# Attention's instruction lists in another order on TensorE, ScalarE and VectorE

## The reference

```python
ln_out = _ln(hidden_states, ln_w, ln_b)
q  = _ln(_fp8_linear_pertensor(ln_out, wq,  ...))      # per head, 128 wide; 16 heads
k  = _ln(_fp8_linear_pertensor(ln_out, wk,  ...))      # 8 groups
v  =     _fp8_linear_pertensor(ln_out, wv,  ...)
core = _gqa(q, k, v)                                    # scores, softmax, values, in batches of 64 rows
qx = _ln(_fp8_linear_pertensor(ln_out, wqx, ...))
kx, vx = split(cond @ w_kv_x);  kx = _ln(kx)
xout = _gqa(qx, kx, vx)
x = x + fp8_linear(concat([core, xout]), wproj)
x = x + moe_ffn(_layernorm(x))                          # router, top 2 of 8 experts, and a shared expert
```

## Time and profile before

| | us |
|---|---|
| median of 3 runs | 1134.46 (1134.02 to 1134.89) |
| the profiled execution | 1130.54 |
| its span | 1128.6 |
| PE busy, share of the span | 989.4, 88% |
| PE weight loads busy | 692.6, 61% |
| DVE busy | 824.0, 73% |
| ACT busy | 716.1, 63% |
| POOL busy | 405.8, 36% |

### The profile page before, as it was taken

The page is one execution under the profiler, slowest core; times in us unless marked ns, Lnnn a source line. Parts: engine busy times, 40 slices in busy tenths (PEclk is TensorE's granted clock), DMA queues, the critical chain, the costliest instruction groups (busy, mean ns, idle before and its releaser), DMA issues. The chain is left out here.

```text
span 1128.6 us, 23597 instructions
## 1 busy us (share of the span) xinstructions
PE 989.4 (88%) x7206; PEld 692.6 (61%) x7207; DVE 824.0 (73%) x1596; ACT 716.1 (63%) x1223; POOL 405.8 (36%) x627
## 2 busy tenths in 40 slices
PE   2447999999999999999999999958999959999994
PEld 1434667667676667666676766746565536666663
DVE  6566888988888888888889888878866634444442
ACT  5967777777777777777777777636455515445452
POOL 3005444444444444444444444400561002332332
PEclk8679999999999999999999999986999979999998
DMA  9245110000100101001010010013453146222222
GB/s 278 50 92 170 43 39 19 27 29 19 37 19 19 37 19 37 19 19 37 19 37 19 19 37 19 1 57 131 150 188 130 56 150 132 28 23 28 28 24 27
DMA packets 32369, 65.20 MB, mean 58 GB/s; under 512 B 3664, under 2 KB 20688, under 8 KB 31952
## 3 DMA queue, kind: packets, MB, share of 16 engines
q1 hardware_dynamic: 23312, 50.20, 13.7%
q0 software_dynamic: 9024, 14.59, 7.6%
HBM read 53.42 MB, written 16.59 MB: 62 GB/s over the span
## 5 line engine op out<-in xcount | busy, mean ns | idle before, releaser
L754 POOL TENSOR_TENSOR root<-vareps,neghalf 128x4 f32<-128x4 f32 (+1 forms) x128 | 169.0, 1320 | 10.0
L747 POOL TENSOR_TENSOR var<-ssq,unit 128x4 f32<-128x4 f32 (+1 forms) x128 | 50.0, 391 | 314.6 <-DVE ssq L659 314.6
L543 PE MATMUL b_pj<-w_hi,xq 128*128 128x512 f16 x384 | 146.6, 382 | 6.6 <-PEq L154 6.3
L559 PE MATMUL b_tr<-ident,nrm 128*128 128x128 f32 x768 | 120.6, 280 | 35.7 <-ACT qT L629 17.4
L543 PE MATMUL b_pj<-w_lo,xq 128*128 128x512 f16 x384 | 146.5, 382 | 0.0
L659 DVE TENSOR_REDUCE ssq<-sq 128x4 f32<-128x512 f32 x192 | 128.5, 681 | 14.9 <-ACT sq L611 14.8
L670 DVE TENSOR_TENSOR nrm<-raw,rstd 128x512 f32<-128x512 f32 x192 | 126.4, 686 | 16.2 <-POOL rstd L758 14.5
L1321 POOL DMA_INDIRECT out<-xg x39 | 60.6, 1553 | 210.7 <-ACT xg L1422 191.4
L559 PEld LDWEIGHTS b_tr<-ident,nrm 128*128 128x128 f32 x768 | 85.5, 146 | 73.0 <-DVE nrm L670 41.0
L569 PEld LDWEIGHTS b_sc<-kT,qT 128*128 128x128 f32 x1024 | 124.3, 192 | 9.3 <-ACT qT L629 0.3
L569 PE MATMUL b_sc<-kT,qT 128*128 128x64 f32 x1024 | 121.3, 272 | 0.0
(11 more groups left out here) (258 smaller groups left out, 2260.8 us busy)
## 6 DMA issues: line engine op xcount, KB each, us to landing
nst<-in_ffw SPq DMA_DIRECT2D x30, 512.0 KB, 3.3
wload<-in_ffw SPq DMA_DIRECT2D x30, 512.0 KB, 3.4
xbuf<-zero SPq DMA_DIRECT2D x39, 129.0 KB, 2.5
xg<-xbuf SPq DMA_DIRECT2D x9, 516.0 KB, 4.2
w<-in_w_all POOLq DMA_DIRECT2D x12, 256.0 KB, 9.2
x_sb<-in_x SPq DMA_DIRECT2D x4, 512.0 KB, 6.8
cstage<-in_ctxT SPq DMA_DIRECT2D x1, 2048.0 KB, 9.6
w<-in_w_all SPq DMA_DIRECT2D x4, 512.0 KB, 14.8
```

The source lines that it names most:

```text
L543: last = pe.matmul(o, a[:, k, bass.ts(i, P)], w[:, k, at:at + BANK], start=(k == 0 and n_ == 0), stop=(k == KT - 1 and n_ == len(terms) - 1))
L559: last = pe.transpose(o, nrm[:, c, hd * P:(hd + 1) * P], ident[:, :])
L754: pool.tensor_tensor(root[:, r % 2, c, :], vareps[:, r % 2, c, :], neghalf[:, 0:1].unsqueeze(2).to_broadcast(shape), ALU.pow).then_inc(s[" ...
```

## The change

Five things are changed, all in the attention.

- PE's list: `pe_probT(0)` moves from behind the second transposes to between the first two projections; `pe_project(2)` moves ahead of the third transposes, so `pe_values` stands directly ahead of the third projection.
- ACT's list: squares and raw copies are separate steps (`act_square` is new), so that `act_exp` stands behind the first raw copy, `act_tev(1)` between the second square and its raw copy, and `act_tev(2)` and `act_ptev` between the third square and its raw copy. The last two copies close the list. `act_weight_squares` goes from the middle to the front and from item N to item N-3.
- DVE's list: `dve_norm(1)` goes ahead of `dve_sub`; `dve_sum` between the first two sums of squares; `dve_cat` and the third sum of squares ahead of `dve_recip`, `dve_norm(0)`, `dve_prob` and `dve_clip`; `dve_round` is last, behind the residual and the statistics, which now belong to item N-3.
- `pe_project` waits for `sq_done` as well (not for c = 1), since a square is no longer always ahead of the copy of another projection.
- `run_slots` runs one slot more at the end, for the steps that are three slots behind.

```diff
--- before.py
+++ after.py
@@ -513,7 +513,7 @@
                         slot(i, r)
                 if before_tail is not None:
                     before_tail()
-                for N in range(4 * (NT - 1), 4 * NT + 2):
+                for N in range(4 * (NT - 1), 4 * NT + 3):
                     slot(N // 4, N % 4)
 
             @block.sync
@@ -531,6 +531,8 @@
                 def step(pe, i, r):
                     n, kind, u = 4 * (4 * i + r) + c, r // 2, r % 2
                     after(pe, "raw_done", n - 1)
+                    if c != 1:
+                        after(pe, "sq_done", NN * (4 * i + r) + max(c - 1, 0))
                     o = b_pj[c % 2][:, :]
                     at = (8 * kind + (u, 2 + 2 * u, 3 + 2 * u, 6 + u)[c]) * BANK
                     if kind == 1 and c in (0, 3):
@@ -600,16 +602,22 @@
                 last.then_inc(s["po_done"], 1)
 
 
+            def act_square(c):
+                def step(act, i, r):
+                    N = 4 * i + r
+                    m = NN * N + c
+                    act.wait_ge(s["proj_done"], 4 * N + c + 1)
+                    after(act, "ssq_done", m - 1)
+                    act.activation(sq[:, (r * NN + c) % 2, :], b_pj[c % 2][:, :], ACT.Square).then_inc(s["sq_done"], 1)
+                return step
+
             def act_raw(c):
                 def step(act, i, r):
                     N = 4 * i + r
                     act.wait_ge(s["proj_done"], 4 * N + c + 1)
                     bk = b_pj[c % 2][:, :]
                     if c < NN:
-                        m = NN * N + c
-                        after(act, "ssq_done", m - 1)
-                        act.activation(sq[:, (r * NN + c) % 2, :], bk, ACT.Square).then_inc(s["sq_done"], 1)
-                        after(act, "norm_done", m - 2 * NN + 1)
+                        after(act, "norm_done", NN * N + c - 2 * NN + 1)
                         act.activation(raw[:, r % 2, c, :], bk, ACT.Copy).then_inc(s["raw_done"], 1)
                     else:
                         after(act, "pv_done", N - 3)
@@ -762,11 +770,37 @@
 
             @block.tensor
             def _(pe):
-                run_slots(pe, [(1, pe_scores), (2, pe_transpose(0)), (3, pe_project(0)), (3, pe_project(1)), (2, pe_transpose(1)), (0, pe_probT), (-1, pe_values), (2, pe_transpose(2)), (3, pe_project(2)), (-2, pe_out), (3, pe_project(3))])
+                run_slots(pe, [
+                    (1, pe_scores),
+                    (2, pe_transpose(0)),
+                    (3, pe_project(0)),
+                    (0, pe_probT),
+                    (3, pe_project(1)),
+                    (2, pe_transpose(1)),
+                    (-1, pe_values),
+                    (3, pe_project(2)),
+                    (2, pe_transpose(2)),
+                    (-2, pe_out),
+                    (3, pe_project(3)),
+                ])
 
             @block.scalar
             def _(act):
-                run_slots(act, [(2, act_tev(0)), (1, act_exp), (3, act_raw(0)), (3, act_raw(1)), (2, act_tev(1)), (0, act_ptev), (2, act_tev(2)), (0, act_weight_squares), (3, act_raw(2)), (3, act_raw(3))])
+                run_slots(act, [
+                    (-3, act_weight_squares),
+                    (2, act_tev(0)),
+                    (3, act_square(0)),
+                    (3, act_raw(0)),
+                    (1, act_exp),
+                    (3, act_square(1)),
+                    (2, act_tev(1)),
+                    (3, act_raw(1)),
+                    (3, act_square(2)),
+                    (2, act_tev(2)),
+                    (0, act_ptev),
+                    (3, act_raw(2)),
+                    (3, act_raw(3)),
+                ])
 
             @block.vector
             def _(dve):
@@ -774,7 +808,24 @@
                     dve.wait_ge(s["st3_done"], EARLY)
                     moments(dve, range(EARLY))
 
-                run_slots(dve, [(1, dve_max), (1, dve_sub), (2, dve_norm(1)), (2, dve_norm(2)), (3, dve_squares(0)), (3, dve_squares(1)), (1, dve_sum), (1, dve_recip), (1, dve_prob), (-1, dve_cat), (-1, dve_clip), (-1, dve_round), (3, dve_squares(2)), (3, dve_norm(0)), (-2, dve_residual), (-2, dve_stats)], early)
+                run_slots(dve, [
+                    (1, dve_max),
+                    (2, dve_norm(1)),
+                    (1, dve_sub),
+                    (2, dve_norm(2)),
+                    (3, dve_squares(0)),
+                    (1, dve_sum),
+                    (3, dve_squares(1)),
+                    (-1, dve_cat),
+                    (3, dve_squares(2)),
+                    (1, dve_recip),
+                    (3, dve_norm(0)),
+                    (1, dve_prob),
+                    (-1, dve_clip),
+                    (-2, dve_residual),
+                    (-3, dve_stats),
+                    (-1, dve_round),
+                ], early)
                 dve.wait_ge(s["st3_done"], NT)
 
             @block.gpsimd
```

## The result

The changed kernel takes 1085.74 us (median of 4, 1085.58 to 1085.91) against 1134.26 for the kernel before in the same comparison: ratio 0.9579, 95% interval 0.9564 to 0.9595, 48.5 us less. In a later comparison it was 1082.86 against 1131.05, ratio 0.9575 (0.9558 to 0.9592); one of the seven executions of the kernel before took 1649 us there at a granted clock of 0.59 and is not counted. The forecast was 1106.5 with a range of 1099 to 1124: the direction was right, the size was too small by 21 us, and the time lies outside the range.

What follows compares the result with a forecast made beforehand. It took a DVE and POOL ring of 10.0 us a slot as the bound; 58 x (10.17 - 9.58) = 34 us, less 6 for short waits, is 28 off 1130.54: 1102.5, as median 1106.5, range 1099 to 1124.

Steps and rivals of the forecast that it cites:

- The ring of DVE and POOL: Attention: POOL's 3.89 us plus DVE's 6.11 from `nrm` to third sum of squares make the 10.0 us slot; 9.29 after.
- POOL's part: From third sum of squares to `nrm`: 3.89 us before, 4.45 after, with POOL held until DVE's `prob` ends.
- the second ring's wait of 17.4 us: PE's transposes waiting for ACT's `qT`; forecast to go, with 0.3 us spare, once a projection lies between.
- rival E: No change, 1134 us: another 10 us ring through exp, square, `qT` and transposes, since `sub` follows a waiting `nrm`; chance 0.05.
- PE's floor after: PE's own work per attention slot after the change: 9.14 us short, 10.00 long, mean 9.58.
- the seam from values to a projection: On PE, in no earlier row, so taken at the 1.24 us of values to transposes; 0.1 either way is 6 us.
- The reserve of 0.1 us a slot: Attention: 6 us of the gain held back for short waits that the timetable does not resolve.
- Filling and draining at nothing, +-3: Both ends of the attention, outside the 58 steady slots: no gain counted, within 3 us either way.
- Rival C: DVE's clip and round hold POOL too: DVE-POOL ring 9.94 us, only 12 us gained, 1123 us; chance 0.20.
- The timetable: Start times within a short slot: norm at 3.33 us in the second, needed by 3.58, so it fits by 0.25.
- Rivals D: Slower, 1145 us: steps moved beside POOL also stretch its `root`; with POOL at 5.5 the slot is 10.35; chance 0.09.
- The edits called free: Side edits expected to cost nothing: probability transposes covered by 2 us; 1.04 us weight squares moved into ACT's 1.49 us wait.

## Why the prediction was too small

**What bounded the kernel before** was half the truth. The ring of DVE and POOL at 10.0 us was there: with DVE's old list no version fell below 1120 except where POOL's part was cut as well (1108). But the ring that set the slot was the other one, through exp, the second `qT` and the third transposes: with 1.43 us cut out of the first, the mean slot stayed at 10.17 (1129.6 us in all), and with the second cut instead, by ACT's list, by PE's, or by both, the first held it at 10.15, 10.09 and 10.03, with PE's weight loads waiting 46 to 52 us for `nrm`. The forecast saw the second ring's wait of 17.4 us and filed it as a minor edit, and gave rival E, which names this ring, 0.05. The price of the whole change was not hurt by that, since it cuts both; any forecast of a part of it from this text would have been wrong, most of all DVE's list alone, 1240 where one ring gives 1107.

**PE's floor after** is the step that failed: forecast 9.14 and 10.00 us, measured 9.01 and 9.87. The term is values, taken at 1.24 from the earlier trace rows, "where nothing is waited for"; it is 1.09. In that row something was waited for. The copy of `qT` ahead of it, in the kernel before:

```profile
464.02 0.80 ACT L629 ACTIVATE qT<-b_tr,col 128x512 f32<-128x512 f32 x1
```

It ends at 464.82, and the transposes start at 464.97, 0.15 behind it. In all 52 slots of the kernel before that were read they start 0.14 or 0.15 behind such a copy, and where they need not wait, with ACT's list alone, they follow values by 1.09 or 1.10. So the 1.24 is 1.09 of values and 0.15 of the wait that the change removes, and the view had no bracket for it. The forecast put its doubt on the seam from values to a projection, at 0.1 to either side; that seam is like the others, and the miss is larger than that bound. The projection behind values takes 0.88 in place of 0.86, which leaves 58 x 0.13 = 7.5 us.

**The reserve of 0.1 us a slot**, 6 us, was for nothing: PE is busy in all of the 548.34 us.

**Filling and draining at nothing, +-3**, was wrong too. Before slot 3 and behind slot 61 another 4.5 + 2.0 us went. The first part is the exchange of third projection and third transposes: with it undone the stretch before slot 3 takes 53.99 us, as long as before (53.52), against 48.92 in the changed kernel measured again. For the second part that exchange does nothing (20.32 us with it undone, 20.09 with it), while PE's whole list undone gives 23.04; which of its entries pays there is open.

28 + 7.5 + 6 + 6.5 = 48, the measured change.

**POOL's part** held: 4.36 us against 4.45, `nrm` and `prob` holding POOL back to back. Rival C fell at the same rows: `root` starts while clip runs and loses 0.07 us beside clip and round. The Trainium skill (GPSIMD Engine Reference, Key points) names instructions in a two-port mode beside those with two SBUF inputs; the kind with two SBUF inputs held POOL here, clip and round did not hold it back. Whether clip and round ran in such a mode is not shown. The timetable was on the safe side: 0.25 us to spare ahead of the second transposes was forecast, and it is 0.50 in the second short slot (scores at 458.54, `nrm` at 461.63, transposes at 462.88, 0.75 needed). Rivals D and E fell with the result. Rival E's ring, through `sub` behind a `nrm` that waits, does exist: it is the 12.4 us of DVE's list alone and the 9.85 of the third transposes put back. In the changed kernel ACT's list and the place of the third projection keep it under PE's 9.01, as the timetable had it.

**The edits called free** were: weight squares, probabilities and `norm` ahead of `sub` change nothing in the changed kernel (1082.7, 1084.1, 1083.7 against 1082.9). Of the change as it is described, what carries it is on PE the third projection ahead of the third transposes, on ACT some part of a list whose old order has exp ahead of all squares and copies of its slot but one, on DVE some part of the list other than the place of `sub`.

## What to carry to other kernels

When an engine waits, follow each of its waits round until the chain comes back to itself, and write down the length of every such ring, also of the one behind the smaller wait: two rings of about 10 us hide each other, and an edit that shortens one may lengthen the other. Before an instruction that waits for a slow neighbour goes ahead of another in a list, ask who hangs on that other: DVE's list alone cost 110 us by this, and 91 of them came back with one exchange. Where the work of the busiest engine is the floor, take each distance between starts from several slots, and look at what the second of the two needs: a row without a bracket is no proof that nothing was waited for. Here one such distance held 0.15 us of wait, in each of 58 slots.

## What was not expected of the hardware

The start of values costs PE 0.09 us more than that of the other groups, behind transposes (0.53 against 0.44) as behind a projection (0.31 against 0.22). And the stage behind the attention, unchanged, took 385.5 us from the last statistics in the profiled execution after, 382.0 in that before and 381.9 in the changed kernel's second profile: 3.5 us that the change does not explain, since the changed kernel has both values.
